# Cross attention of a decoder on one core: heads in another order, value matmuls of two units in turn on two column strips, scores over 64 rows

## The reference

```python
B, N, C = x.shape                    # 2, 256, 256; the context has 2 x 512 rows
q = (x @ Wq + bq).reshape(1, B * N, H, hd)
kv = (cond @ Wkv + bkv).reshape(1, -1, 2, H, hd)
k, v = (kv[:, :, 0], kv[:, :, 1])
...
q = _fq_sym(q, axis=-1)
k = _fq_sym(k, axis=-1)
v = _fq_sym(v, axis=2)
attn = jnp.einsum('bhqd,bhkd->bhqk', q, k)
attn = jax.nn.softmax(attn.astype(jnp.float32), axis=-1)
attn = _fq_unsigned(attn, axis=-1)
out = jnp.einsum('bhqk,bhkd->bhqd', attn, v)
out = jnp.transpose(out, (0, 2, 1, 3)).reshape(B, N, C)
return out @ Wp + bp
```

## Time and profile before

| what | value |
| --- | --- |
| median of 3 runs | 533.05 us (531.3 to 534.2) |
| the profiled execution's own time | 532.18 us |
| its span (first to last instruction) | 530.3 us |
| stage 5's loop, first maximum to last value matmul | 296.2 to 408.3 us of the span |
| busy: TensorE / VectorE / ScalarE / GpSimd | 468.0 / 332.7 / 226.9 / 113.5 us |
| mean granted TensorE clock | 0.94 of full |

### The profile page before, as it was taken

How to read it: one execution, slowest core, us unless ns; L and a number is a source line. 1 busy time by engine, 2 the same in 40 slices (tenths; PEclk the granted TensorE clock), 3 DMA queues, 4 the chain that set the end, 5 groups by cost and what they waited for, 6 DMA issues and landing times.

```text
span 530.3 us, 7963 instructions
## 1 busy us (share of the span) xinstructions
PE 468.0 (88%) x2991; PEld 291.3 (55%) x2991; DVE 332.7 (63%) x621; ACT 226.9 (43%) x546; POOL 113.5 (21%) x210
## 2 busy tenths in 40 slices
PE   4786979999997979999963899999997979999994
PEld 1244457666664536666652466667665535555552
DVE  1999348554534268788837799999996462222225
ACT  3142311222223386595511699999986310001000
POOL 8698021522325200000034011111110000000002
PEclk9978897999997989999987599999999699999999
DMA  8920000000000000000000700000001400000001
GB/s 304 309 67 1 1 0 1 0 2 1 0 1 0 1 0 2 2 1 2 1 1 0 301 19 2 3 2 1 2 1 27 134 0 0 1 0 0 0 1 40
DMA packets 9670, 16.32 MB, mean 31 GB/s; under 512 B 1304, under 2 KB 8280, under 8 KB 9304
## 3 DMA queue, kind: packets, MB, share of 16 engines
q1 hardware_dynamic: 9632, 15.82, 8.9%
HBM read 15.29 MB, written 0.52 MB: 30 GB/s over the span
## 4 chain that ended last, share of the span: by engine, by line
PE 68%; DVE 19%; ACT 6%; issue 4%; DMA 1%; POOL 1%; SPq 0%; POOLq 0%; DVEq 0%; ACTq 0%
PE ps L633 17%; PE ps L1038 6%; PE ps L783 5%; PE ps L822 5%; PE ps L833 4%; PE ps L932 4%; PE ps L747 4%; PE ps L952 4%; PE ps L941 4%; PE ps L754 3%; PE ps L852 2%; DVE area_a L1386 2%; ACT area_b L565 2%; PE ps L816 2%; PE ps L724 1%
## 5 line engine op out<-in xcount | busy, mean ns | idle before, releaser
L1386 DVE CUSTOM_DVE_ANT_0 area_a<-ps,zero,small 128x1024 f32<-128x1024 f32 x64 | 80.0, 1273 | 1.3 <-PE ps L932 1.3
L565 ACT ACTIVATE area_b<-area_a,small 128x1024 int16<-128x1024 f32 x64 | 72.9, 1141 | 5.9 <-POOL small L444 5.7
L546 ACT ACTIVATE area_a<-ps,small 128x256 f32<-128x256 f32 (+1 forms) x128 | 51.9, 433 | 30.0 <-DVE small L1278 28.4
L393 POOL TENSOR_SCALAR var_eps<-meanvar 128x1 f32<-128x1 f32 x24 | 6.1, 253 | 252.6 <-DVE meanvar L1136 252.2
L633 PE MATMUL ps<-xT_odd,area_a 128*128 128x512 f32 x128 | 59.4, 609 | 0.0
L1468 DVE TENSOR_TENSOR area_b<-ps,area_b 128x512 f32<-128x512 f32 x16 | 11.0, 689 | 59.3 <-ACT area_b L609 59.3
L609 ACT ACTIVATE area_b<-ps 128x512 f32<-128x512 f32 x16 | 9.6, 597 | 84.6 <-PE ps L633 84.6
L932 PE MATMUL ps<-area_b 128*128 128x512 bf16 x128 | 40.7, 403 | 3.7 <-DVE small L1386 2.9
L941 PEld LDWEIGHTS ps<-ident_b,area_b 128*128 128x128 bf16 x512 | 34.0, 99 | 17.4 <-ACT area_b L565 5.4
L952 PE MATMUL ps<-area_a,area_b 128*32 128x128 bf16 x512 | 39.9, 221 | 1.0 <-ACT area_a L583 0.8
L941 PE MATMUL ps<-ident_b,area_b 128*128 128x128 bf16 x512 | 40.0, 222 | 0.8 <-ACT area_b L565 0.7
(11 more groups left out here) (255 smaller groups left out, 831.0 us busy)
## 6 DMA issues: line engine op xcount, KB each, us to landing
area_a<-in_w_up_dram SPq DMA_DIRECT2D x1, 4096.0 KB, 13.4
area_a<-in_w_down_dram SPq DMA_DIRECT2D x1, 2048.0 KB, 8.6
area_b<-in_idx_row_dram SPq DMA_DIRECT2D x1, 1024.0 KB, 7.2
ctxT<-in_ctxT_dram SPq DMA_DIRECT2D x1, 1024.0 KB, 9.1
ctx_tok<-in_ctx_dram SPq DMA_DIRECT2D x1, 1024.0 KB, 12.8
w_qkv<-in_w_qkv_dram SPq DMA_DIRECT2D x1, 768.0 KB, 5.9
xT_even<-in_xT_dram SPq DMA_DIRECT2D x1, 512.0 KB, 3.8
wkvx<-in_wkvx_dram SPq DMA_DIRECT2D x1, 512.0 KB, 9.9
```

Of the source, the lines that this page charges most:

```text
L546: a = act.activation(p1[:, n % 2, x * nk * P:(x + 1) * nk * P], scores1(n)[:, x * nk * P:(x + 1) * nk * P], ACT.Exp, bias=nmx1[:, n % 2, x ...
L565: act.activation(px[:, u % PX, :], sx[:, u % 3, :], ACT.Exp, bias=nbx[:, u:u + 1], accum_out=zx[:, i, h:h + 1]).then_inc(sem("px_ready"), 1)
L1386: dve.tensor_tensor_reduce(sx[:, u % 3, :], bank(2 * (u % 2), 2), zero[:].broadcast_to([P, B * M]), qsc[:, u // HX, u % HX:u % HX + 1], LO ...
```

## The change: what it does

- `HEADS` gives the heads of a tile in another order, in which neighbours of a pair (units 2m and 2m + 1) write two different strips of 32 partitions: heads 0 and 3, 4 and 7, then 2 and 1, 6 and 5.
- `apply(m)` issues the value matmuls of both units of a pair in turn, 16 in all, at even steps `u` (`m = u // 2 - 1`). Odd steps have no value matmuls. `ox_ps` counts pairs.
- `scores(u)` contracts over the 64 partitions of its own head instead of 128.
- `pTx` has four buffers, two of them in `area_b`; copies wait for the pair before last.
- `evac_sums` moves one unit later in ScalarE's program (u mod 16 = 2 instead of 1).

```diff
--- before.py
+++ after.py
@@ -49,6 +49,7 @@
 LOWEST = -3.0e38
 ROUND = 12582912.0
 STAGES = 6
+HEADS = (0, 3, 4, 7, 2, 1, 6, 5, 8, 11, 12, 15, 10, 9, 14, 13)
 PX = 3
 SHARE = ((1, 3, 5), 7)
 TURN_AT = 1
@@ -215,7 +216,8 @@
         zx, rzx = tiny([TT, HX]), tiny([TT, HX])
 
         sx = carve("a", DC * E1 * 2 * HE, [3, B * M])
-        pTx = carve("a", DC * E1 * 2 * HE + 3 * B * M, [2, KT * P], BF16)
+        pTx = [carve(where, at + k * KT * P // 2, [KT * P], BF16)
+               for where, at in (("a", DC * E1 * 2 * HE + 3 * B * M), ("b", 26 * N)) for k in range(2)]
 
         w_up = carve("a", 0, [DC, 2, E1 * HE])
         w_down = carve("a", DC * E1 * 2 * HE, [NG, D])
@@ -248,6 +250,10 @@
         def by_scalar(u):
 
             return u % SHARE[1] in SHARE[0]
+
+        def unit5(u):
+
+            return u // HX, HEADS[u % HX]
 
         def pTx_ready(eng, u):
 
@@ -320,7 +326,7 @@
                 load("w_up", w_up.rearrange("p c k h -> p (c k h)"), t["w_up"])
 
                 sp.wait_ge(sem("px_ready"), TT * HX)
-                sp.wait_ge(sem("ox_ps"), TT * HX)
+                sp.wait_ge(sem("ox_ps"), TT * HX // 2)
                 load("w_down", w_down, t["w_down"].rearrange("(g p) d -> p g d", p=P))
 
             for i in range(TT):
@@ -557,7 +563,7 @@
                     act.wait_ge(sem("qTx_ps"), c + 1)
                     act.activation(qTx[0:KW, c, 0, :], bank(6 + c % 2)[0:KW, 0:N // 2].bitcast(BF16), ACT.Copy).then_inc(sem("qTx_even"), 1)
                 for u in range(TT * HX):
-                    i, h = divmod(u, HX)
+                    i, h = unit5(u)
                     act.wait_ge(sem("biasx_ready"), u + 1)
                     if u >= PX:
 
@@ -566,9 +572,9 @@
                                    accum_out=zx[:, i, h:h + 1]).then_inc(sem("px_ready"), 1)
                     if u and by_scalar(u - 1):
                         evac_px(u - 1)
-                    if h == 1 and i:
+                    if u % HX == 2 and i:
                         evac_sums(i - 1)
-                    if h == 4 and i:
+                    if u % HX == 4 and i:
                         evac_z(i - 1)
                 if by_scalar(TT * HX - 1):
                     evac_px(TT * HX - 1)
@@ -577,14 +583,14 @@
 
             def evac_px(u):
                 act.wait_ge(sem("pTx_ps"), u + 1)
-                if u >= 2:
-                    act.wait_ge(sem("ox_ps"), u - 1)
-
-                act.activation(pTx[:, u % 2, :], bank(4 + u % 2).bitcast(I16), ACT.Copy).then_inc(sem("pTx_act"), 1)
+                if u >= 4:
+                    act.wait_ge(sem("ox_ps"), u // 2 - 1)
+
+                act.activation(pTx[u % 4], bank(4 + u % 2).bitcast(I16), ACT.Copy).then_inc(sem("pTx_act"), 1)
 
             def evac_sums(i):
 
-                act.wait_ge(sem("ox_ps"), HX * (i + 1))
+                act.wait_ge(sem("ox_ps"), HX // 2 * (i + 1))
                 if i >= 2:
 
                     act.wait_ge(sem("proj5"), i - 1)
@@ -923,14 +929,14 @@
                 units = TT * HX
 
                 def scores(u):
-                    i, h = divmod(u, HX)
+                    i, h = unit5(u)
                     if u >= 2:
 
                         pe.wait_ge(sem("maxx_ready"), u - 1)
-
+                    rows = slice(KW * (h % 2), KW * (h % 2 + 1))
                     for half in range(2):
-                        mm = pe.matmul(bank(2 * (u % 2) + half), qTx[:, h // 2, h % 2, i * P:(i + 1) * P],
-                                       kTx[:, h // 2, half * 512:(half + 1) * 512], start=True, stop=True)
+                        mm = pe.matmul(bank(2 * (u % 2) + half), qTx[rows, h // 2, h % 2, i * P:(i + 1) * P],
+                                       kTx[rows, h // 2, half * 512:(half + 1) * 512], start=True, stop=True)
                     mm.then_inc(sem("sx_ps"), 1)
 
                 def turn(u):
@@ -942,15 +948,19 @@
                                           px[:, u % PX, k * P:(k + 1) * P].bitcast(BF16), ident_b[:])
                     mm.then_inc(sem("pTx_ps"), 1)
 
-                def apply(u):
-
-                    i, h = divmod(u, HX)
-                    pTx_ready(pe, u)
-                    c, pair = divmod(h // 2, P // PAIR)
-                    dst = bank(6 + i % 2)[pair * PAIR:(pair + 1) * PAIR, c * P:(c + 1) * P]
+                def apply(m):
+
+                    two = []
+                    for u in (2 * m, 2 * m + 1):
+                        i, h = unit5(u)
+                        pTx_ready(pe, u)
+                        c, pair = divmod(h // 2, P // PAIR)
+                        two.append((bank(6 + i % 2)[pair * PAIR:(pair + 1) * PAIR, c * P:(c + 1) * P], h, pTx[u % 4]))
+                    first = m % 4 < 2
                     for k in range(KT):
-                        mm = pe.matmul(dst, ivh[:, k * HX + h, :], pTx[:, u % 2, k * P:(k + 1) * P],
-                                       start=h % 2 == 0 and k == 0, stop=h % 2 == 1 and k == KT - 1)
+                        for dst, h, p in two:
+                            mm = pe.matmul(dst, ivh[:, k * HX + h, :], p[:, k * P:(k + 1) * P],
+                                           start=first and k == 0, stop=not first and k == KT - 1)
                     mm.then_inc(sem("ox_ps"), 1)
 
                 def turn_z(i):
@@ -985,11 +995,11 @@
                         spread_z(u // HX - 1)
                     if u > HX and u % HX == 7:
                         project(u // HX - 1)
-                    if u % HX == 1 and u > 2 * HX:
+                    if u % HX == 2 and u > 2 * HX:
 
                         pe.wait_ge(sem("res5_ready"), u // HX - 1)
-                    if u:
-                        apply(u - 1)
+                    if u and u % 2 == 0:
+                        apply(u // 2 - 1)
                 turn_z(TT - 1)
                 spread_z(TT - 1)
                 project(TT - 1)
@@ -1380,19 +1390,20 @@
                 def maximum(u):
 
                     dve.wait_ge(sem("sx_ps"), u + 1)
+                    i, h = unit5(u)
                     if u >= 3:
 
                         dve.wait_ge(sem("px_ready"), u - 2)
                     dve.tensor_tensor_reduce(sx[:, u % 3, :], bank(2 * (u % 2), 2), zero[:].broadcast_to([P, B * M]),
-                                             qsc[:, u // HX, u % HX:u % HX + 1], LOWEST, ALU.add, ALU.max,
+                                             qsc[:, i, h:h + 1], LOWEST, ALU.add, ALU.max,
                                              mxx[:, u:u + 1]).then_inc(sem("maxx_ready"), 1)
 
                 def evacuate(u):
                     dve.wait_ge(sem("pTx_ps"), u + 1)
-                    if u >= 2:
-                        dve.wait_ge(sem("ox_ps"), u - 1)
-
-                    dve.tensor_copy(pTx[:, u % 2, :], bank(4 + u % 2).bitcast(I16)).then_inc(sem("pTx_dve"), 1)
+                    if u >= 4:
+                        dve.wait_ge(sem("ox_ps"), u // 2 - 1)
+
+                    dve.tensor_copy(pTx[u % 4], bank(4 + u % 2).bitcast(I16)).then_inc(sem("pTx_dve"), 1)
 
                 def invert_z(i):
                     dve.wait_ge(sem("px_ready"), HX * (i + 1))
```

## The result

The changed kernel takes 1.0044 times the time of before (95% interval 1.0027 to 1.0061); its executions have a median of 535.84 us against 532.83 in the same rounds. It is slower by some 2.3 us, under the 0.5% that I called the bound, but clear of no change and outside what my sum gave (-0.2). The ratio leaves out executions more than 1.5% above the kernel's fastest: 7 of 21 of the changed kernel's lie there, at 540.5 to 542.2 us, and none of before's. With them in, the medians differ by 3.0 us. The first profile is one of the long ones (542.19 us, span 540.5); a second one, 539.6 us, is nearly as long. A later profile of the same kernel, 534.71 us, span 533.0, is a typical execution, and is read first.

The account below looks back on a forecast made before the run. VectorE was taken to pace stage 5, with TensorE level. A longer path (+2.0 us) and vanished waits (-2.2) summed to -0.2, giving 532.9 us as median, called no change; range 530.0 to 536.0.

Parts of the forecast that it names:

- Three engines level, VectorE the pace: Stage 5: TensorE, VectorE and ScalarE almost equally loaded; VectorE paces at 1.55 us a unit, TensorE 1.54.
- Strips overlap: Value matmuls: the 16 of a pair last as long as 8 before, saving TensorE 0.45 us a pair.
- The fourth rival, no overlap: Value matmuls: strips run one after the other, 16 last 0.9 us; +7 us, 540; chance 0.04.
- A change of shape costs 0.09 to 0.10 and five replace four: TensorE in stage 5: 64-row scores give a pair five array-shape changes instead of four, adding 0.10 us a pair.
- The path, +2.0: Maximum to copy grows from 1.23 to 1.32 us; 27 VectorE copies each wait 0.07 us more, +2.0 us.
- Waits that go, -2.2: VectorE's larger waits for transposes, 2.0 us in five, mostly go as TensorE lightens, with 0.4 in smaller ones: -2.2 us.
- The sum at full clock: Whole kernel: +2.0 and -2.2 make -0.2 us, with the granted clock taken as 1.00 throughout.
- The clock's effect: Behind stage 5 TensorE falls to half clock; the stage's end shifts against that moment by about a us.
- The first rival, no drain,: Scores switch to 64 rows for free, so only the removed waits count: 530.5 us; chance 0.13.
- The second, VectorE without any gap,: VectorE in stage 5 never waits: -3.7 us, 529.3; chance 0.06.
- The third, ScalarE's copies hold the pair up,: Even steps: value matmuls wait for ScalarE's copy, delaying scores and 13 copies: +4 us, 536.9; chance 0.13.
- The range: Whole-kernel time, 530.0 to 536.0 us, holding the forecast and the nearer part of three rivals.

Follow-up runs that it names:

- rows128: The changed kernel with scores over 128 partitions again, all else kept; 0.9965 of the kernel before, median 530.66 us.
- rows64_only: The kernel before with scores over 64 partitions and nothing else of the change; 1.0091 of the kernel before, +4.8 us.
- after_look: The changed kernel, unchanged, run once more for a profile of a typical execution; 534.71 us, span 533.0.
- rows64_late: The changed kernel with scores over 128 partitions for the first 14 units and over 64 for the other 50; 1.0038 of the kernel before.
- the filler: The changed kernel with one more 512-column matmul, its result overwritten, ahead of the transposes of each of the first 8 units; 1.0075 of the kernel before.
- rows64_turn_first: The changed kernel, 64 rows kept, with the transposes of u ahead of the scores of u + 3; 1.0036 of the kernel before.
- strips_seq: The changed kernel with a pair's value matmuls issued one unit after the other instead of in turn; 1.0101 of the kernel before.

## Why the prediction was right or wrong

- **Three engines level, VectorE the pace.** Right. With TensorE lighter, the middle went from 72.0 to 69.9 us (`rows128`) and no further.
- **Strips overlap.** Right: 0.62 us for sixteen, and in sequence 1.0101. The fourth rival, no overlap, is refuted.
- **A change of shape costs 0.09 to 0.10 and five replace four.** Right: 0.53 instead of 0.44, and 1.64 instead of 1.54 a unit in `rows64_only`.
- **The path, +2.0.** The mechanism is right, the size too large. The wait before a copy is 0.13, not 0.12, and seven plain units take 11.23 us (the copies of units 9 and 16 start at 319.00 and 330.23 in `after_look`; 10.92 in `rows128`), as forecast. But not every copy waits. 18 of the 27 are in the middle, and in `after_look` only ten of them wait 0.13; the other eight start 0.02 us or less behind VectorE's slot, and before each of these end-of-tile work of VectorE puts 1.36 to 2.24 us between the two maxima instead of 1.20. That work covers the longer path, which the prediction granted only to its low end. Ten times the 0.10 over `rows128` is 1.0, and the middle grows by 1.1. Scaled to 27 copies it is 1.6. The product 27 x 0.07 is 1.9, too, and not 2.0.
- **Waits that go, -2.2.** Right in the middle: 72.0 to 69.9, where the waits of 1.6 us in four became 0.5 in two. Wrong in the first units: the 0.39 us at 304.17, put down to TensorE's load there, did not go, and `rows128` has 0.53 at 304.54. The clock had just come out of the half in both. Over the whole kernel `rows128` has -1.9 us by its ratio.
- **The sum at full clock** was then -0.2 in the forecast, and the middle of the changed kernel gained 1.0. What turned it to +2.3 is in none of these terms.
- **The step that failed: "The clock's effect is this: behind stage 5 TensorE falls to the half clock", which I let shift about a us.** I priced the clock only behind the stage, and wrote that the granted clock would be 1.00 throughout. In stage 5 itself the head runs at half clock, and how long was a property of the matmuls there. With 64 rows in the first 14 units, and value matmuls in turn, the full clock comes at 311 to 321 us instead of 303 to 305, at the head's cost of 2.7 to 6.3 us. With 64 rows in the last units it falls as early as 399, ahead of the last value matmul; in `rows64_late` this costs 1.3 us in the tail and 1.2 behind over `rows128`. My sum was made at full clock for a stage that begins at half.
- **The first rival, no drain,** is refuted by the 0.53. **The second, VectorE without any gap,** did not come: ten copies of the middle wait. **The third, ScalarE's copies hold the pair up,** is not seen: the middle would have grown by 2 or 3 us. The slower outcome came by neither of the slower rivals, and none had the clock inside the stage.
- **The range** held the medians, 535.84 and 534.68, but by luck: its upper end was made of +2.0, -1.0 and 1.3 of the clock behind the stage, and what came was a gain of 1.0 in the middle and a loss at both ends. The direction was a small loss where I had called none.

What stays open is how the head and the tail act on each other (1.0038 and 1.0039 alone, 1.0026 to 1.0048 together), and why the clock answers to 64-row scores only where the value matmuls go in turn. With both in the stage's first units, six profiles have the full clock 13.9 us or more behind the first maximum, and only the filler's has it early. The seven other profiles have it after 6.6 to 10.0 us. The tail's earlier fall rests on four profiles (399.4 to 405.1) and is missing in two others of like kernels (`after_look`, `rows64_turn_first`), so it is less sure than the late rise.

## What to carry to other kernels

Where a stage begins or ends at the edge of the clock's two levels, a change that makes TensorE lighter must be summed at both levels, and the units at its ends looked at apart from the middle; a version that kept the full-height matmuls there lost nothing. Two strips in turn are worth it when TensorE is level with the bound, and a smaller contraction is not, if its neighbours in the stream have 128 rows. A gain of one engine out of three level ones ends at the next, here after 2 us of 110.

## What the runs showed of the hardware

- A change between 128 and 64 rows costs 0.09 to 0.10 us at full clock (350.11 to 350.64 for two matmuls of 0.22). At half clock, in the head, it is little more. The timeline of the long execution:

```profile
305.62 1.03 PE L938 MATMUL ps<-area_b 64*128 64x512 bf16 x2
306.59 1.03 PE L947 MATMUL ps<-ident_b,area_b 128*128 128x128 bf16 x8
...
310.46 1.03 PE L938 MATMUL ps<-area_b 64*128 64x512 bf16 x2
```

  From scores to transposes it is 0.97 us. With 128-row scores at half clock it is 0.83 to 0.85 (299.59 less 298.76 and 301.29 less 300.44 in the trace of before): a cost of 0.12 to 0.14. So when the clock halves, the cost does not double as the 0.44 of the scores themselves does; it grows by about a third.
- The moment of the full clock followed what the first units of the stage were. Counted from the first maximum it came after 6.6 to 7.7 us with 128-row scores in them, 7.2 with 64 rows and one unit's value matmuls at a time (`rows64_only`), 7.4 with the filler, 10.0 in sequence (`strips_seq`), and 13.9 to 24.0 with 64 rows and value matmuls in turn. TensorE had no wait between its instructions from 302.73 to 319.8 in the long execution, and its granted clock was 0.50 all the while. I had not expected a matmul's rows to move the clock by 17 us.
- Part of the overlap of strips comes without turns: issued one unit after the other, the sixteen value matmuls started within 0.64 us, where twice the 0.40 of eight were to be expected. In turn they started within 0.40. The Trainium skill (TensorE: Matmul & The Clock Gate, Packing small matmuls) has matmuls on different tiles run concurrently, started a few ns apart; the trace agrees: in turn, the two matmuls of a step start 3 to 4 ns apart (349.389 and 349.393).
